# An attention stage laid out by heads: moments and attention as products of two heads each, four beside each other on TensorE's columns

## What is computed

```python
scale = float(D) ** 0.25
qn = _normalize(q) * (scale * temperature)
kn = _normalize(k) * scale
vN = v1 / N                              # v1: a column of ones ahead of v
kv_mod = jnp.einsum('bhni,bhnj,bhne->bhije', kn, kn, vN)
kv = jnp.einsum('bhnd,bhne->bhde', kn, vN)
vsum = jnp.sum(vN, axis=-2)[:, :, None, :]
y = A * jnp.einsum('bhni,bhnj,bhije->bhne', qn, qn, kv_mod) \
    + scale ** 2 * Bc * jnp.einsum('bhnd,bhde->bhne', qn, kv) + scale ** 4 * Cc * vsum
y_norm, y = (y[..., :1], y[..., 1:])
y = y / y_norm
```

## Time and profile before

| | |
|---|---|
| median of 3 runs | 777.17 us (777.17 to 780.46) |
| profiled execution | 778.77 us, of which 776.9 us are the span from the first to the last instruction |
| TensorE busy | 712.7 us, 92% |
| VectorE, ScalarE, GpSimd busy | 542.0, 425.0, 439.9 us |
| TensorE's granted clock over the span | 0.973 of full speed |
| state-space layers | to about 343 us |
| attention, t = 2 to 9 | about 343 to 495 us |
| experts | from there to the end |

### The profile page before, as it was taken

One profiled execution on the slowest core, in us unless ns is written; L12 is line 12 of the kernel. 1 busy time (PEld: TensorE's weight loads), 2 busy tenths in 40 slices (PEclk: granted clock), 3 DMA queues, 4 the chain that ended last, 5 costly groups with the idle time before them and its releaser, 6 DMA issues.

```text
span 776.9 us, 11085 instructions
## 1 busy us (share of the span) xinstructions
PE 712.7 (92%) x3474; PEld 354.0 (46%) x3474; DVE 542.0 (70%) x859; ACT 425.0 (55%) x763; POOL 439.9 (57%) x402
## 2 busy tenths in 40 slices
PE   5699999999999896869999999889999999999997
PEld 2345454544445453327777778523333333333332
DVE  2399899999899898775588888494444545454543
ACT  1788777878786885523455554544343333333342
POOL 1388777877787766845566666234443434343440
PEclk9799999999999997869999999999999999999999
DMA  4365465434444553331000000644944434443400
GB/s 132 128 165 148 128 155 143 123 95 114 111 123 124 132 131 82 80 87 24 2 1 4 3 5 3 128 94 93 183 99 108 99 75 92 107 105 77 89 1 21
DMA packets 30098, 70.20 MB, mean 90 GB/s; under 512 B 4483, under 2 KB 20175, under 8 KB 29647
## 3 DMA queue, kind: packets, MB, share of 16 engines
q1 hardware_dynamic: 29727, 68.77, 36.6%
q10 hardware_dynamic: 304, 0.63, 0.2%
HBM read 66.96 MB, written 2.43 MB: 89 GB/s over the span
## 4 chain that ended last, share of the span: by engine, by line
PE 46%; DVE 8%; issue 1%; ACT 1%; DVEq 0%; ACTq 0%
PE pair L849 22%; PE pair L930 11%; PE pair L790 5%; PE pair L773 3%; PE pair L826 2%; PE pair L813 1%; PE pair L835 1%; PE pair L841 1%; DVE big L1563 1%; DVE big L1567 1%; DVE big L1629 0%; DVE big L1628 0%; DVE big L1575 0%; DVE big L1568 0%; DVE big L1883 0%
## 5 line engine op out<-in xcount | busy, mean ns | idle before, releaser
L1726 DVE TENSOR_TENSOR hidden<-pair,tmp 128x502 f32<-128x502 f32 (+1 forms) x192 | 121.5, 674 | 127.4 <-PE pair L849 102.6
L1857 POOL TENSOR_TENSOR hidden<-xs,big 128x502 f32<-128x502 f32 (+1 forms) x96 | 111.9, 1167 | 163.4 <-PE pair L849 144.0
L1276 ACT ACTIVATE tmp<-pair 128x502 f32<-128x502 f32 (+1 forms) x192 | 102.4, 586 | 154.5 <-PE pair L849 154.5
L1883 POOL TENSOR_TENSOR big<-big 94x512 f32<-94x512 f32 (+3 forms) x120 | 89.2, 781 | 58.2 <-DVE big L1628 58.2
L849 PE MATMUL pair<-xs,w 64*128 64x502 f32 (+1 forms) x384 | 106.5, 631 | 0.0
L849 PE MATMUL pair<-hidden,w 64*128 64x502 f32 (+1 forms) x384 | 97.7, 585 | 4.3 <-DVE hidden L1726 3.3
L1418 DVE TENSOR_TENSOR_SCAN pair<-tmp,pair 128x750 f32<-128x750 f32 (+1 forms) x56 | 95.8, 1712 | 7.9 <-ACT tmp L1020 7.6
L930 PE MATMUL pair<-hidden,w 128*64 128x502 f32 (+1 forms) x384 | 91.1, 596 | 0.0
L1748 POOL TENSOR_TENSOR big<-big,work 128x750 f32<-128x750 f32 (+1 forms) x28 | 45.8, 1634 | 78.4 <-ACT big L994 78.4
L501 PE MATMUL pair<-big,work 128*128 128x512 f32 x112 | 62.2, 638 | 2.1 <-DVE work L1430 2.0
L849 PEld LDWEIGHTS pair<-hidden,w 64*128 64x128 f32 x384 | 36.6, 187 | 50.8 <-issue 46.1
(11 more groups left out here) (189 smaller groups left out, 1235.6 us busy)
## 6 DMA issues: line engine op xcount, KB each, us to landing
big<-dispatched SPq DMA_DIRECT2D x40, 502.0 KB, 6.6
spread<-rowsd SPq DMA_DIRECT2D x48, 375.0 KB, 5.6
spread<-rowsd SPq DMA_DIRECT2D x48, 187.5 KB, 3.3
big<-in_x SPq DMA_DIRECT2D x12, 375.0 KB, 6.3
big<-dispatched SPq DMA_DIRECT2D x8, 498.0 KB, 5.8
spread<-rowsd SPq DMA_DIRECT2D x8, 374.0 KB, 4.9
w<-in_w SPq DMA_DIRECT2D x5, 512.0 KB, 6.7
big<-in_x SPq DMA_DIRECT2D x1, 1500.0 KB, 8.1
```

The lines of the kernel that those rows point to most:

```text
L1276: act.activation(sT[i % 4][:, 0:w], bank[BANK1[i]][:, 0:w], ACT.Silu).then_inc(silu_a, 1)
L1726: v.tensor_tensor(hidT[i % 8][:, 0:hi - lo], bank[BANK2[i]][:, 0:hi - lo], sT[i % 4][:, 0:hi - lo], ALU.mult)\
L1857: pool.tensor_tensor(xw[e % 4][:, 0:hi - lo], xs[:, lo:hi], wx[:, e, 0:hi - lo], ALU.mult)\
L1883: ins = eng.tensor_tensor(dst[:, :, at:at + H * m].rearrange("p u (h d) -> p u h d", d=m), t[:, :, :, 0:m], t[:, :, :, k:D], ALU.mult)
```

## The change

Features are laid out by heads: 36 pair products, 8 channels and a one for each head, HF = 45, and a part is two heads, FT = 90, FTN = 4. q, k and v stand in `qkv` with a one behind each head's 8 channels.

`moments` now loads 32 columns of v (two heads of 9 columns each, with what lies around them) and streams the 90 features of the same two heads; the result of part g goes to the partitions 32g to 32g + 31, so the four parts lie in four column groups of the array. That is 16 products per half. The moments come out with v on the partitions; VectorE takes only what belongs to a head, weighted, in one multiplication with `featw` into `kvT`, a new step `moments_turned` on TensorE brings the features back onto the partitions by two products with the selection `ksel`, and ScalarE copies the result into `kvm`. `attend` is 16 products of 32 columns loaded (16 of one group, and zeros where the other group's stand) and 188 streamed, again in four column groups. `q_features` has four parts in place of three, with four transposes each. All moments share one PSUM bank (4); the fourth part of the features of an even half goes to bank 5, of an odd one to bank 4. `featw` and `ksel` are made on the core by GpSimd instead of loaded, and `wproj` is loaded in eight small pieces.

```diff
@@ -37,9 +37,14 @@
-QUAD = 288
-FEATS = QUAD + 72
-FT, FTN = 120, 3
+QUAD = 36
+HF = QUAD + D + 1
+FEATS = H * HF
+FT, FTN = 2 * HF, H // 2
+VW = 2 * (D + 1)
+VAT = [144 + VW * g - 14 for g in range(FTN)]
...
@@ -200,7 +209,12 @@
-            return attended(n) if f == FTN - 1 else bank[2 + f]
+            return (bank[2], bank[3], attended(n), bank[4 if n % 2 else 5])[f]
+        def of_heads(t, at, count):
+            return t[:, :, at:at + (D + 1) * count].rearrange("p u (h d) -> p u h d", d=D + 1)[:, :, :, 0:D]
...
@@ -777,20 +799,27 @@
                 pe.wait_ge(lin_a, 2 * r + 1)
-                if n % 2:
-                    after(pe, att_v, n - 1)
-                else:
-                    after(pe, kv_v, n - 1)
+                after(pe, kv_a, n)
+                after(pe, qt_a, FTN * n if n % 2 == 0 else 0)
                 for b in range(2):
-                    for f in range(FTN):
-                        for p in range(2):
-                            unit = (2 * (n % 2) + p) * 2 + b
-                            rows = TP - p
-                            at = 65 * (FTN * b + f)
-                            mm = pe.matmul(bank[4 + n % 2][0:FT, at:at + 65],
-                                           kF[r % 2][0:rows, unit, FT * f:FT * f + FT],
-                                           qkv[r % 2][0:rows, unit, 143:208], start=(p == 0), stop=(p == 1))
+                    for p in range(2):
+                        unit = (2 * (n % 2) + p) * 2 + b
+                        rows = TP - p
+                        for g in range(FTN):
+                            mm = pe.matmul(bank[4][32 * g:32 * g + 32, FT * b:FT * b + FT],
+                                           qkv[r % 2][0:rows, unit, VAT[g]:VAT[g] + 32],
+                                           kF[r % 2][0:rows, unit, FT * g:FT * g + FT], start=(p == 0), stop=(p == 1))
                 mm.then_inc(kv_p, 1)
+            def moments_turned(n):
+                pe.wait_ge(fw_g, 3)
+                pe.wait_ge(kt_v, n + 1)
+                for b in range(2):
+                    mm = pe.matmul(bank[4][0:FT, 256 + 128 * b:384 + 128 * b], kvT[:, FT * b:FT * b + FT], ksel[:, :],
+                                   start=True, stop=True)
+                mm.then_inc(kc_p, 1)
...
@@ -803,10 +832,12 @@
-                    if f == FTN - 1:
+                    if f == 2:
...
-                        if n % 2:
-                            pe.wait_ge(kv_v, n + 1)
+                    if f == 3 and n % 2:
+                        pe.wait_ge(kv_a, n + 1)
+                    elif f == 3:
+                        after(pe, att_v, n)
...
@@ -816,16 +847,17 @@
-                pe.wait_ge(kv_v, n + 1)
+                pe.wait_ge(kz_g, 1)
+                pe.wait_ge(kv_a, n + 1)
...
-                    for f in range(FTN):
-                        for b in range(2):
-                            mm = pe.matmul(dst[64 * b:64 * b + 64, TOK * k:TOK * k + TOK],
-                                           kvm[n % 2][:, k, FTN * b + f, :], qT[n % 2][:, f, TOK * b:TOK * b + TOK],
-                                           start=(f == 0), stop=(f == FTN - 1))
+                    for b in range(2):
+                        for g in range(FTN):
+                            mm = pe.matmul(dst[32 * g:32 * g + 32, TOK * k:TOK * k + TOK],
+                                           kvm[n % 2][:, g, k, b:b + 2, :].rearrange("p b c -> p (b c)"),
+                                           qT[n % 2][:, g, TOK * b:TOK * b + TOK], start=(b == 0), stop=(b == 1))
...
@@ -890,6 +922,8 @@
                         project_qkv(qkvs, 3)
+                    if att is not None:
+                        moments_turned(2 * att)
                     if ln2 is not None:
...
@@ -906,6 +940,7 @@
                         q_features(2 * att)
+                        moments_turned(2 * att + 1)
                     if ln2 is not None:
...
@@ -1217,6 +1252,13 @@
+            def moments(n):
+                act.wait_ge(kc_p, n + 1)
+                after(act, at_p, n - 1)
+                src = bank[4][0:FT, 256:512].rearrange("p (b q c) -> p q b c", b=2, c=16)
+                dst = kvm[n % 2].rearrange("p g k b c -> p (g k) b c")[:, :, 0:3:2, :]
+                act.activation(dst, src, ACT.Copy).then_inc(kv_a, 1)
...
@@ -1237,6 +1279,8 @@
                     ln1, qkvs, att, ln2, gate, last = stages(t)
+                    if att is not None:
+                        moments(2 * att)
                     if qkvs is not None:
...
@@ -1247,6 +1291,7 @@
                         q_features(2 * att)
+                        moments(2 * att + 1)
                     if ln2 is not None:
...
@@ -1634,11 +1682,9 @@
                 v.wait_ge(kv_p, n + 1)
-                after(v, at_p, n - 1)
-                src = bank[4 + n % 2][0:FT, 0:2 * FTN * 65].rearrange("p (f c) -> p f c", c=65)
-                v.tensor_tensor(kvm[n % 2][:, 0], src[:, :, 1:65], featw[:, :, :], ALU.mult)
-                v.tensor_tensor(kvm[n % 2][:, 1], src[:, :, 0:1].to_broadcast([FT, 2 * FTN, 64]), featw[:, :, :],
-                                ALU.mult).then_inc(kv_v, 1)
+                after(v, kc_p, n)
+                v.wait_ge(fw_g, 2)
+                v.tensor_tensor(kvT, bank[4][:, 0:2 * FT], featw[:, :], ALU.mult).then_inc(kt_v, 1)
...
@@ -1829,16 +1875,35 @@
-                    pool.memset(t[:, :, 64:72], 1.0)
-                    ins = pool.memset(t[:, :, 136:144], 1.0)
+                    ins = pool.memset(t.rearrange("p u (h d) -> p u h d", d=D + 1)[:, :, :, D:D + 1], 1.0)
...
+                f = featw.rearrange("p (q f) -> p q f", f=HF)
+                pool.memset(f[:, :, 0:D], 0.5)
+                pool.memset(f[:, :, D:QUAD], 1.0)
+                pool.memset(f[:, :, QUAD:QUAD + D], float(D) ** 0.5)
+                pool.memset(f[:, :, QUAD + D:HF], float(D)).then_inc(fw_g, 1)
+                pool.wait_ge(fw_g, 1)
+                pool.wait_ge(hd_v, 1)
+                f = featw.rearrange("p (b h f) -> p b h f", b=2, f=HF)
+                for h in range(2):
+                    ins = pool.tensor_scalar(f[:, :, h, :], f[:, :, h, :], ofhead[:, h:h + 1], None, ALU.mult)
+                ins.then_inc(fw_g, 1)
+                src = ident.rearrange("p (g c) -> p g c", c=32)[:, :, 14:32].rearrange("p g (h d) -> p g h d", h=2)
+                dst = ksel.rearrange("p (g k h d) -> p g k h d", g=FTN, k=2, h=2)
+                pool.tensor_copy(dst[:, :, 0], src[:, :, :, 0:D])
+                pool.tensor_copy(dst[:, :, 1], src[:, :, :, D:D + 1].to_broadcast([128, FTN, 2, D])).then_inc(fw_g, 1)
...
+                for t in kvm:
+                    ins = pool.memset(t[:, :, :, 1, :], 0.0)
+                ins.then_inc(kz_g, 1)
...
-                        return qkv[r % 2][:, :, at:at + 64].rearrange("p u (h d) -> p u h d", d=D)
+                        return of_heads(qkv[r % 2], at, H)
...
@@ -1880,9 +1945,9 @@
-        ins = eng.tensor_tensor(dst[:, :, at:at + H * m].rearrange("p u (h d) -> p u h d", d=m),
+        ins = eng.tensor_tensor(dst.rearrange("p u (h f) -> p u h f", f=HF)[:, :, :, at:at + m],
...
-        at += H * m
+        at += m
```

46 lines of the change are left out of this document (29 added, 17 removed).

## The result

The changed kernel takes 775.89 us (median of 15 runs, 772.87 to 778.42), the kernel before 778.56 us (15 runs, 777.1 to 783.45). The ratio is 0.9956, 95% interval 0.9938 to 0.9974: faster, by 3.4 us by the ratio (2.7 between the medians), where 6.5 were forecast. A second comparison gave 0.9934 (0.9908 to 0.9960). The forecast gain of 0.83% (a ratio of 0.9917) lies outside the first interval and near the edge of the second.

What follows compares the result with a forecast made beforehand. The attention stage was taken as bound by a chain from TensorE to VectorE, both near their limit. Terms -4.0 - 0.4 - 1.1 - 2.3 + 1.3 = -6.5 us from the median 777.17 gave 770.7 us, range 764.5 to 781.

Steps and rivals of the forecast that it cites:

- items 1 to 5: Prices per half: moments save 1.65 us, attention 0.65, VectorE's masking 0.63; transposes cost 0.32 more, turning 0.45.
- item 1: Moment block on TensorE: 0.85 us for 32 records, ends 0.64 and 2.6; 2.0 by the skill's 62 ns.
- Item 4: New turning of the moments on TensorE: 0.45 us per half, up to 0.7 with the load in the open.
- Item 5: VectorE's masking: two multiplies become one of 180 elements at 0.3 us, saving 0.63 us per half.
- items 6, 7: ScalarE's added copies cost 0.7 us per half; GpSimd's 16 products stay at 12.04 us, 30% more as other end.
- rival (b): Contention: strided GpSimd writes lengthen VectorE's small masks, or ScalarE's new copies cost 0.5 us each; 776 us, chance 0.21.
- A full period: Periods t = 4 to 7: everything behind the second normalization comes 1.0 us earlier, 18.35 us each, -4.0 us together.
- It waits half a microsecond: In a full period VectorE, ready at 11.7 us, waits at the second normalization for ScalarE's second deviation, ending at 12.25.
- rival (c): TensorE's savings come through: -1.6 us in six periods, -2.3 in t = 9, nothing in t = 2; 765 us, chance 0.13.
- t = 3 and t = 8: Attention-stage periods: t = 3, with copies costing 1.4 us against TensorE's 2.9, gains 0.4; t = 8, ending on ScalarE's copies, 1.1.
- t = 9: Last attention period: TensorE saves 2.9 us, less 0.55 us of turning waiting in the open, so -2.3 us.
- t = 2: First attention period: the mask behind VectorE's query products delays ScalarE's squares, norms and copies; +1.3 us, ends -0.5 and +3.

Runs made afterwards that it cites:

- e8: Changed kernel, t = 2 squares before the moments' copy, dummy products in t = 2 and 8, t = 9 turning behind projection, second deviation earlier: 769.00 us, ratio 0.9853.
- e1: The kernel before, run again with no edit: ratio 0.9987.
- e5: Changed kernel with unread products on TensorE, seven at the end of t = 8 and four in t = 9: 770.31 us, ratio 0.9879.
- e10: As e8 without the deviation move, with VectorE's first mask ahead of the query products and eight dummies ahead of t = 2's transposes: 769.10 us, ratio 0.9856.
- e11: Kernel before with three unread ScalarE instructions in t = 8 ahead of the last feature copies: 789.51 us, ratio 1.0114.
- e12: Kernel before with the three ScalarE instructions of e11 plus eleven dummy TensorE products ahead of t = 8's last attention products: 779.96 us, ratio 1.0001.
- e6: Changed kernel with ScalarE's squares in t = 2 moved ahead of its copy of the turned moments: ratio 0.9931.
- e2: The changed kernel, run again with no edit: ratio 0.9934.
- e9: Changed kernel with VectorE's first mask in t = 2 moved ahead of the query products: 772.74 us, ratio 0.9897.
- e4: Kernel before with the change's new constants and weight pieces built and loaded but not used: ratio 1.0000.

## Why the prediction was wrong, step by step

- **The prices of the products** (items 1 to 5): right. The two bounds of item 1 were 0.64 and 2.6 us; 0.83 was measured, and the 2.0 us that stood beside them did not appear. Item 4 took 0.60 instead of 0.45, with its tail. Item 5 is 0.35 us for an instruction (0.3).
- **ScalarE and GpSimd** (items 6, 7): right. L1254 takes 1.58 us for four copies, where 1.24 for three and 0.38 more make 1.62. The copy L1261 lasts 0.38 to 0.40 us and holds the queue for 0.27. GpSimd is busy 11.99 us in a full period, 12.04 before, and VectorE's first small mask beside it takes 0.84 us (L1615), where 0.91 stood. No contention was added, and rival (b) is out.
- **A full period**: the mechanism was right and one size off. The norms end 8.54 us into the period (8.55 forecast) and VectorE's L1675 starts at 8.57 (8.6). "It waits half a microsecond" failed. ScalarE's L1223 ends 3.13 us behind the norms, not 3.7: the second layer norm's squares L1216 now start as the norms end and the transposes are there, so that the 0.87 us between the norms' end and the first copy (431.74 to 432.61) became 0.27. VectorE waits a tenth of a microsecond. So the period lost 1.6 us, not 1.0, as rival (c) had it. Three engines now arrive at about the same time: the chain runs over TensorE's transposes and ScalarE's copies, as forecast, and VectorE's own way to this place (11.7 us, as forecast) is as long. In e8 ScalarE was 0.3 us earlier still and the chain merely went through the norms and VectorE.
- **t = 3 and t = 8**: by the same failure, -1.65 and -1.7 instead of -0.4 and -1.1. In t = 3 TensorE's busy time fell by 2.67 us (17.59 to 14.92), and 1.65 of them came through; I had let the copies take 1.4 and waits the rest.
- **t = 9, the step that failed**: "-2.9 + 0.55 = -2.3" became +2.1. The sum took all products at the full clock. What the forecast did not ask is what a TensorE with less to do does to its clock. The last attention products of t = 8 wait 2.00 us where they had waited 1.48 in e1, and the clock fell for 10.20 us. With TensorE kept busy there t = 9 is 14.2 to 14.4 us (e5, e8, e10). So the clock costs 3.3 to 3.5 us and the rest of the step is -1.3, not -2.3. Half of that last difference is the wait ahead of the turning, 1.09 us where 0.55 was forecast; the other half was not followed up. That TensorE's idle time brings the clock down, and not something else in the new products, is shown from both sides: e5 fills it after the change; e11 makes more of it, and e12 fills that, in the kernel before.
- **t = 2, the same failure**: +1.3 became +3.1, by another way than I gave. ScalarE's squares came late as forecast (10.1 us into the period, forecast 10.4) and did not matter (e6). TensorE waits 3.21 us ahead of the turning, for VectorE's mask, and the low clock that follows is the cost: with TensorE kept busy in the wait and the rest as in e6, t = 2 is 19.34 us (e8), a little less than the 19.70 to 19.87 of the kernel before. The kernel before ran both blocks of moments in one go while VectorE made the query products. Now the first turning stands ahead of the second block, and since the moments of both halves share one bank, that block waits for mask, turning and copy of the first. I had followed ScalarE's queue past this edit and not TensorE's. A second bank for the moments was not tried.
- **The sum**: -4.5 us in place of -6.5. The steady part gave 4.3 us more than forecast (-9.75 against -5.5), and t = 2 and t = 9 took 6.2 more. Had only the clock in t = 9 stayed up, the table would give -8; e5, which kept it up, is 9.4 us below the kernel before by its ratio, and its profile shows 7.6 of them in the stage (141.9 us against 149.5). With the clock kept up in t = 2 as well it was 11 us (e8, e10), more than was forecast. The range (764.5 to 781) held the time, but in part by luck: a full period that gained more than forecast stood against two falls of the clock that the forecast did not have.

## What to carry to other kernels

Where TensorE gets faster at a place where another engine sets the end, ask how long it now stands idle and what the granted clock does behind that: here an expected gain turned into a loss of 2 us, and eleven products that nobody reads (e5) brought about as much as the whole change. Narrow products in four column groups paid here since consecutive products go to different groups: the same products, one group after another, take more than twice as long. Ahead of a change that gives two buffers' work to one, follow the queue of the engine that filled them, not only that of the one with the new instruction.

## What the runs showed of the hardware that was not expected

- A wait of 2.00 us at the end of t = 8 was followed by 10.20 us at 0.50 of the clock (after and e2; some 13.6 us in e9); the old kernel's 1.48 us at the same place was not (before, e1, e4). With a wait of 2.71 us in the old kernel the fall lasted 3.40 us in the one run that was profiled.
- The length of one wait does not settle it. In t = 2 of the old kernel the clock fell behind a wait of 1.53 us in the first profile and stayed up behind one of 1.78 us in e1; in e9 it fell in t = 2 with no single wait over 0.92 us.
- Issued in turn over four column groups, 32 records of 90 columns take 0.83 us (0.026 us each) and 32 of 188 columns 1.48; issued one group after another, 1.84 and 3.46. The floor of 0.08 us per record that the earlier trace rows left possible is not one, even in one group (0.058).
- Transposes of 94 columns take the same time per record with 90 columns loaded (16 in 1.46 us) as with 120 (12 in 1.13).
